# Masked cross-attention and MoE-FFN layer on one core: the order in which SP issues its transfers

## The reference

```python
x = x + attn(ctx_1024, layernorm(x), mask)      # sim = q k^T * scale, masked, softmax, @ v, @ Wo
# in attn: kv_in = concat([layernorm(ctx), lat]); alphas = softmax(where(mask, sim, -inf))
# in ffn:  scores = sigmoid(xt @ gate_w); top 2, normed to sum 1 -> dense [T, 8]
#          y = sum_e dense[:, e] * (silu(xt @ w1[e]) * (xt @ w3[e])) @ w2[e]  + shared expert
x = x + ffn(layernorm(x))
```

## Time and profile before

| | |
|---|---|
| three runs | 1152.14, 1158.64, 1159.47 us (median 1158.64) |
| profiled execution | 1153.85 us, its span 1152.1 us |
| PE busy | 1083.4 us (94%) |
| DVE busy | 926.4 us (80%) |
| ACT busy | 792.1 us (69%) |
| POOL busy | 615.2 us (53%) |
| DMA | 176.81 MB, mean 153 GB/s |
| granted TensorE clock, mean | 0.989 |

### The profile page before, as it was taken

How to read it: one execution, slowest core, us unless ns; L and a number is a source line. 1 busy time by engine, 2 the same in 40 slices (tenths; PEclk the granted TensorE clock), 3 DMA queues, 4 the chain that set the end, 5 groups by cost and what they waited for, 6 DMA issues and landing times.

```text
span 1152.1 us, 28179 instructions
## 1 busy us (share of the span) xinstructions
PE 1083.4 (94%) x7720; PEld 941.8 (82%) x7720; DVE 926.4 (80%) x4095; ACT 792.1 (69%) x2924; POOL 615.2 (53%) x717
## 2 busy tenths in 40 slices
PE   6899999999999999999999999999999999999976
PEld 6788887888888788888888888888888888888755
DVE  3878887888887788888888888778888788888756
ACT  4887777776777677777776677776777776777631
POOL 5555555555555455555555555555555555554421
PEclk9999999999999999999999999999999999999979
DMA  5455455555455555455555555555455555545531
GB/s 153 141 165 155 152 169 161 163 153 154 150 170 155 162 147 159 145 172 161 171 155 154 154 158 170 168 152 149 137 168 168 168 151 154 155 149 163 157 117 33
DMA packets 248717, 176.81 MB, mean 153 GB/s; under 512 B 29424, under 2 KB 215408, under 8 KB 248560
## 3 DMA queue, kind: packets, MB, share of 16 engines
q1 hardware_dynamic: 247376, 173.96, 50.8%
q10 hardware_dynamic: 1184, 1.05, 0.3%
HBM read 103.35 MB, written 71.56 MB: 152 GB/s over the span
## 4 chain that ended last, share of the span: by engine, by line
SPq 26%; PE 24%; DVE 21%; DMA 11%; issue 11%; ACT 5%; POOL 0%; DVEq 0%; POOLq 0%; ACTq 0%
SPq L335 13%; DMA pT<-probsT_dram 9%; SPq L363 6%; PE bank L860 5%; PE bank L873 4%; PE bank L815 4%; PE bank L817 3%; PE bank L816 3%; SPq L328 3%; DVE logits L671 3%; DVE probsT L686 3%; ACT probs L557 3%; SPq L369 3%; DVE h L704 2%; DVE g_eq L603 2%
## 5 line engine op out<-in xcount | busy, mean ns | idle before, releaser
L453 POOL TENSOR_TENSOR probs<-probs,rdenom 128x512 f32<-128x512 f32 x256 | 266.4, 1041 | 405.0 <-DVE rdenom L680 400.4
L557 ACT ACTIVATE probs<-logits,neg_max 128x128 f32<-128x128 f32 x1024 | 398.7, 396 | 0.9 <-DVE neg_max L671 0.9
L873 PEld LDWEIGHTS bank<-kvT,tT 128*128 128x128 f32 x2048 | 268.8, 192 | 120.3 <-issue 106.8
L860 PE MATMUL bank<-pT,kv_f 128*128 128x512 f32 x512 | 269.3, 607 | 44.2 <-DMA pT<-probsT_dram 43.9
L873 PE MATMUL bank<-kvT,tT 128*128 128x128 f32 x2048 | 270.7, 275 | 0.0
L716 DVE TENSOR_TENSOR cT_lo<-bank,cT_hi 128x512 fp32r<-128x512 f32 x256 | 175.2, 685 | 83.8 <-ACT cT_hi L527 83.7
L671 DVE CUSTOM_DVE_ANT_0 logits<-bank,mask_add 128x128 f32<-128x128 f32 x1024 | 232.6, 282 | 6.1 <-PE bank L873 5.9
L527 ACT CAST cT_hi<-bank 128x512 fp32r<-128x512 f32 x256 | 150.0, 586 | 113.1 <-PE bank L860 112.5
L557 ACT ACTIVATION_READ_ACCUMULATOR probs<-logits,neg_max 128x1 f32 x1024 | 197.6, 193 | 0.0
L512 ACT ACTIVATE h_tanh<-bank 128x256 f32<-128x256 f32 x160 | 61.6, 385 | 180.7 <-PE bank L817 178.3
L686 DVE STREAM_TRANSPOSE probsT<-probs 128x512 f32<-128x512 f32 x256 | 176.0, 688 | 0.7 <-issue 0.5
(11 more groups left out here) (102 smaller groups left out, 1996.4 us busy)
## 6 DMA issues: line engine op xcount, KB each, us to landing
probsT_dram<-probsT SPq DMA_DIRECT2D x256, 256.0 KB, 2.4
pT<-probsT_dram SPq DMA_DIRECT2D x1024, 64.0 KB, 2.2
gates<-gates_dram SPq DMA_DIRECT2D x62, 256.0 KB, 4.2
kv_raw<-in_ctx SPq DMA_DIRECT2D x32, 128.0 KB, 2.8
kv_raw<-in_x SPq DMA_DIRECT2D x32, 128.0 KB, 2.9
mask_raw<-in_mask_BxS_ik SPq DMA_DIRECT2D x32, 128.0 KB, 3.4
x_res<-in_x SPq DMA_DIRECT2D x32, 128.0 KB, 2.7
out<-out_sb SPq DMA_DIRECT2D x32, 128.0 KB, 3.0
```

What stands on the lines that cost most here:

```text
L453: nc.gpsimd.tensor_tensor(by_pair, by_pair, rdenom[n][:, :].unsqueeze(2).unsqueeze(3).broadcast_to([P, PAIRS, P // QUAD, QUAD]), ALU.mult) ...
L557: nc.scalar.activation(probs[c % 4][:, :, r, :], logits[c % 2][:, r, :].rearrange("p (c k) -> p c k", k=QUAD), ACT.Exp, bias=neg_max[c % 2 ...
L860: nc.tensor.matmul(C_ps[c % 2][:, :], kv_f[g % 3][:, kl % 4, :], pT[c % 3][:, :], start=True, stop=True).then_inc(C_in_psum, 1)
L873: last = nc.tensor.matmul(S_ps[c % 2][:, P * r:P * (r + 1)], tT[:, kl % 4, hd:hd + 2, :], kvT[g % 2][:, kl % 4, :], start=True, stop=True)
```

## The change: what SP issues in which order

In each step k, the loads of half e - 2 now stand in front of the store of half e - 1, and the frame's own transfers stand in front of both. These are spread: gate loads from k = 6 to k = 0 of the next frame, the mask from k = 0 to k = 1, `x_res` from k = 1 to k = 2, the output from k = 0 to k = 3, the four gate stores two each to k = 5 and k = 6, `kv_raw` from k = 0 to k = 7 of the frame before. Number, sizes and semaphores of the transfers stay as they were. The other four engines' programs are the same.

```diff
                 for k in range(HALVES):
                     e = HALVES * i + k
-                    if has_half(e - 1):
-                        store_probs(e - 1)
-                    if has_half(e - 2):
-                        load_probs(e - 2)
-                    if k == 0 and has(j, p, -1, NG - 3):
-                        load_kv(j, p + 2)
+                    if k == 0 and has(j, p, 3, NG + 1):
+                        sp.wait_ge(gates_stored, 64 * (i - 2))
+                        after(sp, h_routed_done, NT * (i - 3))
+                        for a in range(2):
+                            sp.dma_start(gates[FH * a:FH * (a + 1), :, :],
...
+                    if k == 1 and has(j, p, -1, NG - 3):
                         load_mask(j, p + 2)
-                    if k == 0 and has(j, p, 4, NG + 2):
-                        store_out(i - 1)
-                    if k == 1 and has(j, p, 0, NG - 1):
+                    if k == 2 and has(j, p, 0, NG - 1):
...
+                    if k == 3 and has(j, p, 4, NG + 2):
+                        store_out(i - 1)
+                    if k in (5, 6) and has(j, p, 2, NG):
...
                         sp.wait_ge(gate_step, GATE_STEPS * (i - 1))
                         after(sp, gates_loaded, 32 * (i - 2))
-                        for a in range(P // QUAD):
+                        for a in (0, 1) if k == 5 else (2, 3):
...
+                    if k == 7 and has(j, p, -2, NG - 4):
+                        load_kv(j, p + 3)
+                    if has_half(e - 2):
+                        load_probs(e - 2)
+                    if has_half(e - 1):
+                        store_probs(e - 1)
```

## The result

The changed kernel takes 1213.96 us in the median of four runs (1212.78 to 1218.87), the kernel before 1157.64 beside it. The ratio is 1.050, with a 95% interval from 1.046 to 1.055: five per cent slower. The profiled execution of after has a span of 1211.5 us, where before had 1152.1. The forecast was 1188 us, in a range of 1150 to 1225.

What follows compares the result with a forecast made beforehand. SP's transfers were on the path, with PE idle 43.9 us for pT. Rounds of 35.0 us per full frame summed to 1112.8, putting the last product 31 us later: 1185 or 1190, forecast 1188 us, range 1150 to 1225.

Steps and rivals of the forecast that it cites:

- The closed round: On SP's queue, store, landing, four loads and next store run in series and set the pace, 4.3 to 4.5 us.
- The clean round of 4.0 us: One undisturbed SP round: landing 2.15, four loads 1.74, gap 0.10 us; eight are 32.0 us per frame.
- The break-even of 4.24 us: SP round length at which line 860's last product would start at 1122.0 us, as before the change.
- Long issues, 0.13 per group: Some SP load issues take one to two us instead of 0.43, adding 1.05 us per frame.
- Gate loads, 0.9: The store behind the gate loads on SP lands later, adding 0.9 us per frame.
- kv, mask, x_res and out, 0.2 each: Each of these transfers delays the landing of the store behind it, adding 0.8 us per frame in all.
- Late landings with no neighbour, 0.25 per frame: Stores that land late without gate loads or other bulky transfers ahead add 0.25 us per frame.
- The gate wait moved ahead of the loads, nothing: First gate stores wait for gates ahead of SP's loads, 1.9 us late if punctual; counted as nothing since SP runs late.
- At most 43.9 us to be given back: PE's idle time before line 860, waiting for pT, is the most a better transfer order can return.
- Rival 1: SP's round runs clean, a frame takes 32.9 us and PE is the bound: 1110 to 1125 us; chance 0.15.
- Rival 2: SP's mean round is 4.24 us and PE's waits only move elsewhere: about 1155 to 1160 us; chance 0.13.
- Rival 3: Late stores hold up DVE's transposes, then logits and PE: 31 to 62 us on top, 1216 to 1247; chance 0.06.

Runs made afterwards that it cites:

- the pair of runs with one order each: One extra 16 KB store per half behind the four loads: in the changed kernel 1302.33 us, in the kernel before 1199.51 us.
- The run with small gates: The changed kernel with gate loads cut to a quarter of their bytes, computing less than the reference: 1186.33 us.
- the spread alone: The changed kernel with the store of half e - 1 again in front of the loads of half e - 2: 1108.82 us, ratio 0.959.

## Why the prediction was right, and where it was off

The direction, the mechanism and the range were right, the size was not: 31 us more were forecast, and the medians differ by 56. At 1213.96 us the kernel came out at the top of the forecast's own range (1168 to 1215), whose upper bound was worked out for a landing of 2.4 us in every round and 0.9 us more per frame, 2.51 on average; 2.47 was measured. The forecast's 1188 was 26 us short.

- **The closed round sets the pace.** Right: the chain, the waits, and the pair of runs with one order each. Of 0.52 us more in SP's round, 0.36 show. As foretold, SP's wait for landings came in many pieces (231), the first frame was already slow (35.4 us), and PE's wait spread over seven of the eight places of a frame.
- **The clean round of 4.0 us.** Right: 2.13 + 1.73 + 0.10 = 3.96 us at 756.59. The price of a store right behind loads, taken from single stores of the old trace, carried over.
- **The break-even of 4.24 us.** It stood close to the clean round, and the sum of the unclean rounds decided. Measured is 4.46, where the sum gave 1112.8 / 255 = 4.36. (The 33.6 us of the first two frames don't follow from the terms, which leave 33.9 without gates and output; that is 0.6 us in all.) Line 861's last product started at 1181.2 instead of the 1152.9 worked out. Of these 28 us, 25 are rounds, 1.7 a later first store (36.2 instead of 34.6), 1.4 a longer way from the last store to the product (6.9 instead of 5.5).
- **Long issues, 0.13 per group.** Right: groups average 1.88 us against 1.74. Nothing hid them.
- **Gate loads, 0.9.** Right: 0.97 above a clean 2.15. The run with small gates gave 0.84 back.
- **kv, mask, x_res and out, 0.2 each.** Wrong: in full frames the stores behind them landed after 2.23 to 2.49 us on average, those of k = 4 to 6, with nothing or two gate stores ahead, after 2.31 to 2.41. Without those that meet an instruction packet it is 2.15 to 2.24 and 2.19 to 2.26. They cost nothing of their own that can be seen.
- **Late landings with no neighbour, 0.25 per frame.** This is the term that was mis-sized. The landings exceed 2.15 by 80.8 us in sum, 2.5 per frame, where the prediction had 1.95 with all three landing terms; that makes about 21 of the 25 us that the rounds took longer than the sum. The first frames, which have no gates, took 35.4 and 35.0 us instead of 33.6. The prediction had seen the long issues and taken the late landings for the effect of neighbours; both are mostly PE's instruction fetches, which were in the old trace too (62 packets there as here), where SP waited only 21.8 us for landings in all.
- **The gate wait moved ahead of the loads, nothing.** Right: SP waited for the gates once in after, 6.3 us, at 1186.3, behind the last round. Stores were 4.8 us behind their transposes at that place, more than the 1.9 to be covered.
- **Gate loads hidden from POOL.** Right: POOL waited twice, 9.6 us, both times at the end of the program (1176.2 and 1195.4).
- **PE waits most in k = 5.** Right in substance, wrong in name: the halves at place 5 of a frame are meant (117 and 125 in the two rows). SP loads them in k = 7, right behind the gate loads, and PE multiplies them in its own step k = 1.
- **At most 43.9 us to be given back.** Too low: the spread alone gave 47, since PE's busy time fell too. The bound counted idle time alone.
- **Rival 1, the faster outcome.** It needed long issues that fall where SP waits. In a closed order they don't: they are part of the round. But its second half, that PE's stalls behind the gate loads vanish, came true where the round stays open: the spread alone is 47 us faster.
- **Rival 2, no change.** It needed a mean round of 4.24 us; 4.46 was measured.
- **Rival 3, DVE held up.** The wait came (100.6 us) and cost nothing clear of the noise.

## What to carry to other kernels

Before a wait is put directly behind the transfer that it waits for, add up the round on the issuing queue: landing plus issues plus gaps, by its mean and not by its median, and compare it with the time that a step of the pipeline has. Here the open order (this store, then the loads of the one before) left SP waiting 12.5 to 21.8 us for landings in all, the closed one 280.7. A change with two parts is worth taking apart: here the half that spreads bulky transfers over the steps was a gain of four per cent, and the other half hid it.

## What the runs showed of the hardware

A fetch of PE's instructions shows in the DMA view as one packet of 16 KB and took 0.9 to 1.8 us in after. Where one falls into a closed round, the round is about 1 us longer: 5.12 us instead of 4.14, and with 21 fetches fewer the 255 rounds were 18.6 us shorter. In before there are 62 too; what they cost in the open order, no run tells. Which of the 16 engines carries it, and whether a transfer that avoids that engine would go free, no run here tells.
